# A graph network kernel on one core: layer 0 sums source groups as their counts land, and the far mask is turned from the same blocks

## The reference, cut to what matters

```python
    def _L0_gnn_ref(x, edge_index, W_gcn, b_gcn, W_V):
        ...
        norm = dinv[src] * dinv[dst]
        msg = XW[src] * norm[:, None]
        z_local = jax.ops.segment_sum(msg, dst, num_segments=n) + b_gcn
        HtH = H.T @ H
        z_global = beta / n * (H @ HtH @ W_V)
        out = jax.nn.relu(z_local + z_global)
        return l2_normalize_rows(out)
    def _gat_conv(x, W, a_src, a_dst, b, src, dst, n):
        xw = x @ W
        e = jax.nn.leaky_relu((xw @ a_src)[src] + (xw @ a_dst)[dst], 0.2)
        m = jax.ops.segment_max(e, dst, num_segments=n)
        ex = jnp.exp(e - m[dst])
        ...
    x = x + _L0_gnn_ref(_layernorm(x, axis=-1), edge_index, ...)
    x = x + _L0_ffn_ref(_layernorm(x, axis=-1)[None], ...)[0]
    x = x + _L1_gnn_ref(_layernorm(x, axis=-1), edge_index, ...)
```

## Time and profile before

| | |
|---|---|
| median of 3 runs | 6018.67 us (6018.44 to 6023.18) |
| the profiled execution, its own time | 6056.71 us |
| its span on the core | 6054.7 us |
| mean granted TensorE clock | 0.852 of 2.4 GHz |
| PE busy | 4210.3 us (70%) |
| DVE busy | 3163.7 us (52%) |
| ACT busy | 2049.5 us (34%) |
| POOL busy | 1720.5 us (28%) |
| DMA | 733.45 MB, mean 121 GB/s |

### The profile page before, as it was taken

The page is one execution under the profiler, slowest core; times in us unless marked ns, Lnnn a source line. Parts: engine busy times, 40 slices in busy tenths (PEclk is TensorE's granted clock), DMA queues, the critical chain, the costliest instruction groups (busy, mean ns, idle before and its releaser), DMA issues. The chain is left out here.

```text
span 6054.7 us, 59140 instructions
## 1 busy us (share of the span) xinstructions
PE 4210.3 (70%) x17905; PEld 2780.9 (46%) x17905; DVE 3163.7 (52%) x6104; ACT 2049.5 (34%) x3990; POOL 1720.5 (28%) x1889
## 2 busy tenths in 40 slices
PE   1240037897477395879998599899499397988557
PEld 1130025675211374767776322322377365766356
DVE  8533025212697645972112798997598345453413
ACT  5100000212387103542222388788365211011212
POOL 1366665565575661100000121211011110000142
PEclk9975568998688697998999699899699698999778
DMA  9400025115343463540000244443254334553276
GB/s 383 181 1 1 0 88 185 58 39 156 114 152 103 142 217 126 194 120 10 0 0 22 82 162 146 139 157 123 96 193 143 114 104 138 188 163 108 90 202 208
DMA packets 464216, 733.45 MB, mean 121 GB/s; under 512 B 131537, under 2 KB 258767, under 8 KB 457149
## 3 DMA queue, kind: packets, MB, share of 16 engines
q1 hardware_dynamic: 420524, 710.67, 35.4%
q0 software_dynamic: 43408, 19.43, 1.3%
HBM read 587.26 MB, written 147.32 MB: 121 GB/s over the span
## 5 line engine op out<-in xcount | busy, mean ns | idle before, releaser
L1226 PE MATMUL l2g_a_agg_acc<-all_x,l2g_a_h 128*65 128x512 f32 (+1 forms) x1400 | 651.0, 591 | 23.9 <-ACT l2g_a_agg_flat L1251 21.1
L399 POOL DMA_INDIRECT far<-all_nil,all_far_cell x416 | 496.1, 1192 | 300.2 <-DMA far<-all_nil,all_far_cell 149.6
L399 POOL DMA_INDIRECT table<-first_count,first_cell x416 | 407.0, 978 | 411.1 <-issue 281.4
L1324 DVE SCALAR_TENSOR_TENSOR all_x<-all_x,l2g_a_agg_counts 128x512 f32<-128x512 f32 (+1 forms) x700 | 404.7, 625 | 123.2 <-ACT all_x L1274 122.7
L1263 ACT ACTIVATE l2g_a_agg_z<-l2g_a_agg_z 128x512 f32<-128x512 f32 (+1 forms) x700 | 344.3, 538 | 148.0 <-PE l2g_a_agg_z L1206 123.5
L883 PE MATMUL l0g_agg_acc<-l0g_agg_halves,l0g_agg_exact 128*128 128x512 f32 x625 | 154.0, 401 | 338.9 <-DVE l0g_agg_exact L936 334.6
L1274 ACT ACTIVATE all_x<-l2g_a_agg_z 128x512 f32<-128x512 f32 (+1 forms) x700 | 353.7, 569 | 0.0
L883 PE MATMUL l3g_agg_acc<-l3g_agg_halves,l3g_agg_exact 128*128 128x512 f32 x1250 | 303.8, 397 | 52.5 <-DVE l3g_agg_exact L936 47.5
L1818 DVE SCALAR_TENSOR_TENSOR all_x<-l1f_moe_py,l1f_gate,all_x 128x256 f32 x200 | 96.7, 484 | 440.0 <-PE l1f_moe_py L1775 440.0
L399 POOL DMA_INDIRECT table<-all_count,all_cell x256 | 260.3, 1017 | 166.2 <-DMA table<-all_count,all_cell 76.5
L1226 PEld LDWEIGHTS l2g_a_agg_acc<-all_x,l2g_a_h 128*65 128x65 f32 x1400 | 173.2, 147 | 286.9 <-issue 207.8
(11 more groups left out here) (790 smaller groups left out, 9094.8 us busy)
## 6 DMA issues: line engine op xcount, KB each, us to landing
l3g_agg_counts<-table SPq DMA_DIRECT2D x250, 320.0 KB
...
l2g_a_agg_mask<-far SPq DMA_DIRECT2D x50, 800.0 KB, 4.4
l1g_gat_agg_counts<-table SPq DMA_DIRECT2D x150, 256.0 KB
l2g_b_agg_counts<-table SPq DMA_DIRECT2D x150, 256.0 KB
```

Of the source, the lines that this page charges most:

```text
L399: pool.indirect_dma_start(self.table, bass.IndirectOffsetOnAxis(ap=self.cell[:, b, p:p + 1], axis=0), self.count(b, p), None, bounds_check ...
L1226: pe.matmul(to, rhs(t, r * per + h), p[:, u % n_p, 0:n], start=(t == 0), stop=(t == nt - 1), skip_group_check=True).then_inc(summed, 1)
L1324: dve.scalar_tensor_tensor(out=w, in0=w, scalar=1.0, in1=counts[:, b % n_counts, 0:n], op0=ALU.min, op1=ALU.mult).then_inc(weighted, 1)
```

## The change

1. `scatter1` no longer ends in "sort2". That stage runs columns 134 to 216, the other 200 run inside the new `l0g_agg`, which is `aggregate_as_landed`. This goes through 25 units (source group outside, destination group inside), 5 source tiles and 5 destination tiles each. SP waits before each source group until the number of landed windows (`landed_groups`, counted up by POOL) covers the rows of the group; that number is computed from the sorted keys (`reach`, in `sort_edges` and in the stage "dinv"). The last group waits for all 52 windows.
2. The sums of each unit are added into `z` in SBUF by DVE (10 instructions for each of 25 units, instead of for each of 5 groups).
3. From the same `exact` blocks PE turns 25 pieces per unit into two PSUM banks, ACT makes relu(1 - count) of them as bfloat16 (7 instructions a unit), DVE multiplies by -1e30 (one instruction of [128 x 3200] a unit), and a DMA of ACT's queue writes the 0.8 MB into `far1`. The 416 columns of `scatter_far` and the 73 DMAs that filled `far1` are gone.
4. `scatter2` moves later: 24 columns in `l0g_agg`, 12 in `l0g_end`, 12 in `l0f_ln`, 208 in `l0f_moe`.

```diff
@@ sort_edges
-            mark(dve.scalar_tensor_tensor(out=o.same[:], in0=key, scalar=-1.0, in1=o.same[:], op0=ALU.mult, op1=ALU.add))
-            mark(dve.scalar_tensor_tensor(out=dst, in0=dst, scalar=float(o.n_pad), in1=src, op0=ALU.mult, op1=ALU.add))
-            dve.wait_ge(step, n)
-            mark(dve.tensor_tensor(dst, dst, o.same[:], ALU.add))
+            for g in range(T // G1 - 1):
+                mark(dve.tensor_scalar(flag, key, float((g + 1) * G1 * P * o.n_pad), None, ALU.is_lt))
+                dve.wait_ge(step, n)
+                mark(dve.tensor_reduce(reach[:, g:g + 1], flag, AX, ALU.add))
+                dve.wait_ge(step, n)
...
-            dve.wait_ge(cells_ps, 2)
-            dve.tensor_copy(turned_cell[:].rearrange("p b n -> p (b n)"), pt[:, 0, 0:w]).then_inc(cells_ready, 1)
@@ Scatter.run
             if i == 0 and k >= self.open:
                 pool.wait_ge(self.landed[(k - self.open) % 2], 16 * self.window * ((k - self.open) // 2 + 1))
+                if progress is not None:
+                    pool.sem_inc(progress, k if j == start else 1)
...
+            if progress is not None:
+                pool.sem_inc(progress, 1)
@@ aggregate_as_landed (new)
+    n_ring, n_exact = 5, 2 * G1
+    n_quads = -(-G1 * G1 // 4)
+    units = [(sg, dg) for sg in range(ng) for dg in range(ng)]
...
+                for u, (sg, dg) in enumerate(units):
+                    if dg == 0 and sg + 1 < ng:
+                        sp.wait_ge(landed_groups, sp.value_load(c.reach_groups[0:1, sg:sg + 1], min_val=1,
+                                                                max_val=filling.n // filling.window))
+                    elif dg == 0:
+                        sp.wait_ge(landed_groups, filling.n // filling.window)
+                    for kk in range(G1):
+                        i, k = u * G1 + kk, sg * G1 + kk
+                        if i >= n_ring:
+                            sp.wait_ge(counts_set, i - n_ring + 1)
+                        sp.dma_start(counts[:, i % n_ring, :], table2[k * P:(k + 1) * P, dg * cols:(dg + 1) * cols]
+                                     ).then_inc(counts_in[i % n_ring], 16)
...
+                filling.run(pool, start, filling.n, landed_groups)
+                scatter, first, last = nexts
+                scatter.run(pool, first, last)
...
+                    for q in range(n_quads):
+                        n = (min(4 * q + 4, G1 * G1) - 4 * q) * P
+                        act.wait_ge(quad_ps, u * n_quads + q + 1)
+                        act.activation(mask[:, u % 2, q * 512:q * 512 + n], pt[:, (u * n_quads + q) % 2, 0:n], ACT.Relu,
+                                       bias=unit[:, 0:1], scale=-1.0).then_inc(quad_read, 1)
+                    if u:
+                        store_mask(u - 1)
...
+                        for j in range(G1):
+                            if kk == 0 and u:
+                                pe.wait_ge(sums_free, (u - 1) * G1 + j + 1)
+                            end = kk == G1 - 1 and sg > 0
+                            last = pe.matmul(acc[:, j, :], exact[:, i % n_exact, j * P:(j + 1) * P], halves[:, k, :],
+                                             start=(kk == 0), stop=end, skip_group_check=True)
...
+                    for q in range(n_quads):
+                        at = u * n_quads + q
+                        if at >= 2:
+                            pe.wait_ge(quad_read, at - 1)
...
+                            last = pe.transpose(pt[:, at % 2, (piece - 4 * q) * P:(piece - 4 * q + 1) * P],
+                                                exact[:, (u * G1 + kk) % n_exact, j * P:(j + 1) * P].bitcast(F32), c.ident[:])
...
+                def make_mask(u):
+                    dve.wait_ge(quad_read, (u + 1) * n_quads)
+                    dve.tensor_scalar(mask[:, u % 2, :], mask[:, u % 2, :], FAR, None, ALU.mult).then_inc(masked, 1)
@@ build, l0_gnn and l0_ffn
-                scatter1.run(pool, at[-1], scatter1.n)
+                scatter1.run(pool, at[-1], behind_sort)
...
-    aggregate(nc, "l0g_agg", c, table, h, z, scale=dinv, plus=True, beside=(scatter, 0, 104))
+    aggregate_as_landed(nc, "l0g_agg", c, table, far, h, z, dinv, *filling, (scatter, 0, 24))
...
-            experts_apart(nc, "l0f_moe", xt, ne, w1, b1, w2, b2, parts, [(cells2, 128, cells2.n), (far_cells, 0, 104)])
+            experts_apart(nc, "l0f_moe", xt, ne, w1, b1, w2, b2, parts, [(cells2, 48, cells2.n)])
...
-                tail=lambda t: agg[:, t, :], n_counts=10, lag=5, ring=16, beside_h=(far_cells, 150, 162),
-                beside=(far_cells, 162, 258))
+                tail=lambda t: agg[:, t, :], n_counts=10, lag=5, ring=16)
...
-        add_parts(nc, "l0f_add", x, gate, parts, ne, beside=(far_cells, 258, 280))
+        add_parts(nc, "l0f_add", x, gate, parts, ne)
...
-            aggregate(nc, "l1g_agg", c, tables[0], h, agg, scale=dinv, beside=(scatters[1], 306, scatters[1].n))
+            aggregate(nc, "l1g_agg", c, tables[0], h, agg, scale=dinv)
```

195 lines of the change are left out of this document (148 added, 47 removed).

## The result

| | before | changed |
|---|---|---|
| median of 4 runs | 6020.93 us (6018.44 to 6033.17) | 5839.03 us (5837.30 to 5843.96) |
| the profiled execution, its span | 6054.7 us | 5842.2 us |
| mean granted TensorE clock | 0.852 | 0.874 |
| POOL busy | 1720.5 us | 1240.1 us |
| ACT busy | 2049.5 us | 2150.2 us |

The ratio is 0.9695, 95% interval 0.9678 to 0.9712: 182 us less, where 140 were forecast; 5839 lies inside the range, near its low end, but outside the 5850 to 5925 that the prediction gave its forecast, and 8 us from rival D's 5831.

The account below looks back on a forecast made before the run. Between 550 and 852 us the kernel was taken as bound by graph 1's 282 columns alone. Gains of 77 + 21 + 14 + 28 = 140 off 6056.7, less 38 to the median, gave 5879 us, range 5825 to 5950.

Parts of the forecast that it names:

- rival D: Whole kernel: windows hold the idle pace of 11.93 us and l0f_gat_agg gives nearly all 38; 188 gained, 5831 us, chance 12%.
- The start, the columns' pace, the unit: l0g_agg: columns start at 550 us, 25 windows of 13.4 us make 335, a unit takes 10.3 us.
- the 77: l0g_agg: the stage ends at 952 us instead of 1029.3, 77 us gained.
- 3.7 from the stage's first load to the first product: l0g_agg, behind the last landing: 3.7 us pass before the last five units' first product.
- The clock: l0g_agg, last five units: 2 us for the low clock after idling, five products taking 2.50 instead of 1.3 us.
- Rival B: l0g_agg: DVE's instructions hold up POOL's columns, 17 us a window; 50 us gained in all, 5969 us, chance 15%.
- I take 13.4, since the same clamps and takes run on DVE: l0g_agg: graph 1's windows take 13.4 us each, as graph 2's did in the old l0g_agg.
- at most 0.5 and 2 us: l0g_agg, by the skill's port rule: clamps delay a column by at most 0.5 us, the mask's multiplication by 2.
- Rivals C and E: l0g_agg: C, 21.1 us a window, 6071 us, chance 3%; E, groups find their windows only at the end, 6034, 2%.
- m2 ... lose columns that no wait shows; 0: m2, l0f_gat_h, l1g_ln and l1g_w: losing columns gains 0 each, up to 3 us together.
- behind l0g_agg, with no column late, 8.84: Behind l1g_agg: PE's wait falls from 22.6 us to the 8.84 seen behind l0g_agg, 14 gained.
- l0f_add: l0f_add: DVE's 24.47 us idle before the next stage falls to 3 to 4 without columns, 21 gained.

Follow-up runs that it names:

- Run 3: Changed kernel, but SP waits for all 52 windows before the first unit; ratio 0.9973 to the kernel before, 167 us slower than the changed kernel.
- run 7: Changed kernel, but before source groups 3 and 4 DVE takes the previous unit's sums and makes its mask ahead of its wait; 5833.06 us, ratio 0.9683.
- run 4: Changed kernel without the mask's arithmetic (no turns, relu or multiplication; stores write zeros); ratio 0.9696 to the kernel before.
- run 9: Kernel without turns, relu and multiplication, with the clamps of the counts also made by ACT as plain copies; l0g_end begins at 938.1 us.
- run 1: Kernel before without the far mask's 416 columns, graph 1's columns and the sum unchanged; 5958.97 us, ratio 0.9827.
- run 2: Kernel before with no far-mask columns in m2 alone, those behind moved up and the last 46 left out; ratio 0.9965, 21 us less.
- run 12: The kernel before again, unchanged, for its trace; 6057.59 us.

## Why the prediction was right, and where it was short

**The start, the columns' pace, the unit: right.** 25 windows took 336 us from the first column to the last landing, 335 + 3 were forecast; but the 13.4 is a mean of two paces, 14.4 beside units (15 windows) and 12.2 without (10). A unit was 10.2 for 10.3. Run 3 gives the early start by itself: without it the whole change would be worth 0.3%.

**The end of l0g_agg: the 77 is right in part by luck.** The forecast set the end of the stage's work, the last store counted in, at 952; in the changed kernel that store is issued at 955.1 and takes some 4 us (the median to landing is 3.8 for the last three), so it is through at about 959.5, 7 to 8 us late: the work of the stage ended 70 us earlier than before, not 77. 2 of the 7 to 8 are the later last landing. The others lie in the step "3.7 from the stage's first load to the first product": it took 10.5, as DVE takes the sums of the previous unit only behind the new clamps (run 7, where it takes 3.5). The clock (1.8: 25 products in 7.72 instead of 5.93), the five units and the tail of about 10 were as forecast. What made up for the 7 to 8 us was a term that the sum does not have, the barrier behind the stage: l0g_end began 8.84 us behind the last work in the kernel before and about 1 behind the last store in the changed one, since POOL was through with its 24 columns at 931.

**Rival B, DVE holds POOL up: real, but small here.** The step "I take 13.4, since the same clamps and takes run on DVE" used the right row without its cause. In the l0g_agg of before, from which it comes, 90 of the 104 columns lie beside a `tensor_scalar` and take 1.04 us on average: clamps that come singly delay them little. Runs 4 and 9 show the cause: a column beside a train of DVE's `tensor_scalar` waits, one beside the take of sums from PSUM does not. Of the 36 us that the columns lose to the units (run 3) waits for landings make 22 to 25 and issuing 11 to 14, by the windows of the changed kernel's two traces against those of run 3. The Trainium skill's rule ("SBUF — State Buffer", Who interferes with whom) names `tensor_scalar` among the instructions that can lock GpSimd out, and the traces agree in which columns wait. The prediction held "at most 0.5 and 2 us" a column by it; in run 4 a column that takes 0.97 alone took up to 3.4 behind a train of five clamps, because it waited for the whole train. Rival B's 17 us a window came true only in that run (17.1 on average up to 708 us). Of run 4 one learns that turns taken off PE are not time taken off the unit: PE's wait for the sums and a lower granted clock took most of it back, and the DVE trains pushed the last landing back by 19 us, twice what the shorter units behind it saved.

**Rival D named the number (5831), not the way.** Windows beside units did not go at 11.93, and l0f_gat_agg gave 28.3 of 38: PE's waits for POOL went down by 37.5, as D had it, but 15.2 us of waits for DVE came in their place.

**Rivals C and E did not occur:** no window took 19 us, and SP loaded for group 3 from 772.9 us on (forecast 767), not at the end.

**The 34 us that the sum lacked** are mostly in steps that the prediction set at nothing or read from the wrong row. (1) "m2 ... lose columns that no wait shows; 0": 16.7. Two signs were in the trace of before and were not read, POOL's first column of m2 and PE's first turn there:

```profile
1449.75 0.97 POOL L399 DMA_INDIRECT far<-all_nil,all_far_cell  x1 [10.61 <-POOLq L58]
...
1455.66 1.75 PE L563 MATMUL m_pt<-all_ident,m_panel 128*128 128x128 f32 x7 [18.75 <-DMA m_panel<-table]
```

PE began m2 18.75 us behind its last product, and POOL's next column stood 10.61 behind its last one of l0f_moe. The columns that l0f_moe still issued at its end set the barrier (gone in run 1, still there in run 2, 16.2), and m2's own columns its length (run 2). The same sentence set l1g_ln and l1g_w at 0; they gave 2.2. (2) "behind l0g_agg, with no column late, 8.84": POOL's last column there was issued at 1027.9, just before DVE's last instruction ended at 1029.3, so the row was no barrier without columns. Without any, PE began l1g_t 1.1 us behind DVE's last instruction of l1g_agg (0.8 in run 1), where 8.84 was taken; the term was 21.7 instead of 14. That of l0f_add was 24.1 instead of 21, as DVE waited 0.8 and not 3 to 4. (3) The 2.7 of l0f_ln stay open, as said above.

**The base.** The 38 us between the profiled execution and the median were taken off as a constant. That fits: 33.5 us, the difference of the two first traces in front of l3f_moe, lie where the change does nothing (run 12). But no execution of before near the median was traced, so it isn't shown that these 33.5 are the ones that the median lacks.
